# A graph network kernel: early sums cut into even pieces, row search spread out, and unread products on TensorE between the row search and the first transposes

## The reference, cut to what matters

```python
h = relu(layernorm(x))
h = relu(h @ enc_w1.T + enc_b1) @ enc_w2.T + enc_b2
for w in conv_w:                       # 5 layers
    agg = segment_sum((h @ w)[src], dst)
    r, z, n = gates(agg, h)            # a GRU cell, 128 wide
    h = (1 - z) * n + z * h
x = x + sigmoid(relu(relu(h) @ dec_w1.T + dec_b1) @ dec_w2.T + dec_b2)
h = relu(layernorm(x))
x = x + norm_adj @ relu((norm_adj @ h) @ W1.T + b1) @ W2.T + b2
```

## Time and profile before

| | |
|---|---|
| time, median of 3 runs | 748.6 us (747.67 to 749.78) |
| the profiled execution's own time | 747.64 us |
| its span, first to last instruction | 745.6 us |
| PE busy | 722.0 us (97%), 4078 instructions |
| DVE busy | 334.5 us (45%) |
| ACT busy | 314.4 us (42%) |
| POOL busy | 46.3 us (6%) |
| mean granted clock of TensorE | 0.993 of full |

### The profile page before, as it was taken

How to read it: one execution, slowest core, us unless ns; L and a number is a source line. 1 busy time by engine, 2 the same in 40 slices (tenths; PEclk the granted TensorE clock), 3 DMA queues, 4 the chain that set the end, 5 groups by cost and what they waited for, 6 DMA issues and landing times.

```text
span 745.6 us, 9909 instructions
## 1 busy us (share of the span) xinstructions
PE 722.0 (97%) x4078; PEld 393.7 (53%) x4078; DVE 334.5 (45%) x675; ACT 314.4 (42%) x461; POOL 46.3 (6%) x55
## 2 busy tenths in 40 slices
PE   5899999999999999999999999999999999999997
PEld 3566666445444444444444444544445545558886
DVE  7999998434013332122331222656644631122432
ACT  3978777655334444234462333432446411112000
POOL 6320000000000000000000000120002220000000
PEclk7999999999999999999999999999999999999999
DMA  5120000743202232021240212620002000000100
GB/s 165 26 75 2 1 1 2 135 80 62 37 1 47 52 61 53 1 49 37 45 84 0 48 37 38 94 83 2 1 0 85 20 1 1 1 1 2 37 30 26
DMA packets 78795, 28.40 MB, mean 38 GB/s; under 512 B 70340, under 2 KB 77893, under 8 KB 78618
## 3 DMA queue, kind: packets, MB, share of 16 engines
q1 hardware_dynamic: 77786, 26.93, 17.1%
q0 software_dynamic: 240, 0.66, 0.3%
q10 hardware_dynamic: 720, 0.13, 0.1%
HBM read 8.03 MB, written 2.60 MB: 14 GB/s over the span
## 4 chain that ended last, share of the span: by engine, by line
PE 81%; DVE 12%; ACT 2%; DMA 2%; SPq 1%; POOL 1%; issue 1%; ACTq 0%; DVEq 0%
PE PSA L1207 35%; PE PSA L1426 8%; DVE CT L839 6%; PE PSA L1290 5%; PE PSA L1370 5%; PE PSA L1221 3%; PE PSA L1230 3%; PE PSA L1229 3%; PE PSA L1223 3%; PE PSA L1225 3%; PE PSA L1232 3%; PE PSA L1153 2%; PE PSA L1358 2%; PE PSA L1346 1%; DVE stat L804 1%; ACT AT L1533 1%
## 5 line engine op out<-in xcount | busy, mean ns | idle before, releaser
L1207 PE MATMUL PSA<-AT,H 128*128 128x512 fp8e3 (+1 forms) x1472 | 276.0, 347 | 0.8 <-DMA H<-H 0.6
L1207 PEld LDWEIGHTS PSA<-AT,H 128*128 128x128 f16 x1472 | 126.7, 98 | 152.2 <-issue 13.1
L1045 DVE SCALAR_TENSOR_TENSOR rS<-PSA,bias,rS 128x512 f32<-128x512 f32 (+1 forms) x35 | 23.9, 682 | 265.7 <-ACT rS L1600 265.7
L1600 ACT ACTIVATE rS<-PSA,bias 128x512 f32<-128x512 f32 (+1 forms) x35 | 22.1, 632 | 199.6 <-PE PSA L1229 199.6
L839 DVE TENSOR_TENSOR CT<-CT 128x2048 bf16<-128x2048 bf16 x80 | 91.3, 1204 | 0.1
L1533 ACT ACTIVATE AT<-PSA 128x1000 fp8e3<-128x1000 f32 (+1 forms) x79 | 74.4, 1000 | 23.0 <-PE PSA L1153 23.0
L1507 ACT ACTIVATE CTL<-AT 128x3125 fp8e3<-128x3125 fp8e3 (+1 forms) x25 | 69.9, 2796 | 0.0
L1370 PE MATMUL PSA<-CT,H 128*128 128x512 fp8e3 (+1 forms) x336 | 65.5, 352 | 0.3 <-POOL H L747 0.3
L1426 PE MATMUL PSA<-AT,CT 128*128 128x256 f16 x576 | 65.1, 273 | 0.6 <-DVE AT L1007 0.6
L1426 PEld LDWEIGHTS PSA<-AT,CT 128*128 128x128 fp8e3 x576 | 55.4, 98 | 7.3 <-DVE AT L1007 0.8
L1290 PE MATMUL PSA<-AT,H 128*128 128x512 fp8e3 x250 | 59.0, 379 | 0.0
(11 more groups left out here) (173 smaller groups left out, 660.6 us busy)
## 6 DMA issues: line engine op xcount, KB each, us to landing
AT<-scale_scratch SPq DMA_DIRECT2D x1, 1562.5 KB, 6.5
H<-in_x SPq DMA_DIRECT2D x1, 1536.0 KB
out<-AT SPq DMA_DIRECT2D x12, 128.0 KB
comb_scratch<-CT SPq DMA_DIRECT2D x1, 960.0 KB, 5.2
comb<-comb_scratch SPq DMA_DIRECT2D x5, 192.0 KB, 3.0
H<-yS SPq DMA_TRANSPOSE x48, 2.5
H<-in_x SPq DMA_DIRECT2D x1, 512.0 KB, 5.1
CT<-AT SPq DMA_TRANSPOSE x25, 4.0
```

The source lines that it names most:

```text
L1207: last = nc.tensor.matmul(bank[:, 0:w], H16[:, l % 2, t, h, :], AT3[:, t, n0:n0 + w], start=(t == 0 and h == 0), stop=(t == T - 1 and (h = ...
```

## The change

Eight edits are in it:

1. **Unread products.** TensorE makes matmuls of 512 columns on an index row and writes them to a bank that nobody reads: 512 and 384 columns at the start (512 and 512 before), four more between the row search and the first transposes of keys, two more between these and the first transposes of x.
2. **Row search spread out.** Of the 5 groups only k = 0 and 1 are finished at the start. ScalarE copies the products of k = 2 to 4 (`kept`), and VectorE finishes them behind the one-hots of batches 7, 11 and 15 (`ROWS_AT`). The compares are cut in 128, 128 and 384 windows, in place of 128 and 512. The gathers of k = 2 to 4 come later on GpSimd.
3. **Keys later.** `KEYS_AT` is 5, 12, 20, 28 (before 5, 11, 17, 23).
4. **Even pieces.** `PART` cuts the early sums of chunks 2 and 3 in 4, 3, 4, 3, 4, 3, 4 tiles, and of chunk 1 partly in 3.
5. **Tail tile in layer 0.** Its two halves lie in one matmul in layer 0 too: ScalarE writes the encoded last tile twice side by side (`tail_twice`), one transpose brings it to rows 0 to 52 and 64 to 116.
6. **Copies of the tail rows** are made chunk by chunk, 7 times two DMAs, as the chunks fill, ahead of the 5 transposes of `AT` in SyncE's queue, each pair waiting for the pair before it to land.
7. **The copy in layer 0** behind chunk 5 goes away.
8. **The end.** SyncE's wait for the stores comes behind the branch on the flag.

```diff
-        KEYS_AT = {5: 1, 11: 2, 17: 3, 23: 4}
+        KEYS_AT = {5: 1, 12: 2, 20: 3, 28: 4}
+        ROWS_AT = {7: 2, 11: 3, 15: 4}
...
+        EVEN = [0, 4, 7, 11, 14, 18, 21, T]
+        PART.update({23 + 7 * i + g: [(2 + i, EVEN[g], EVEN[g + 1])] for i in range(2) for g in range(7)})
...
-            sp.wait_ge(window_bank_free, NGR)
+            for c in range(NC):
+                n0, w = CH[c][0] * P, width(c)
+                sp.wait_ge(window_bank_free, min(filled(n0 + w), NGR))
+                if c >= 1:
+                    sp.wait_ge(tail_doubled, 32 * c)
+                for p0, p1 in ((0, LR // 16 * 16), (LR // 16 * 16, LR)):
+                    sp.dma_start(AT3[64 + p0:64 + p1, FT, n0:n0 + w], AT3[p0:p1, FT, n0:n0 + w]).then_inc(tail_doubled, 16)
...
-                    if l == 0 and c == 5:
-                        sp.wait_ge(sum_ready, NC)
-                        for p0, p1 in ((0, LR // 16 * 16), (LR // 16 * 16, LR)):
-                            sp.dma_start(AT3[64 + p0:64 + p1, FT, :], AT3[p0:p1, FT, :]).then_inc(tail_doubled, 16)
...
-            sp.wait_ge(output_stored, 16 * (FG + 2))
             sp.wait_ge(flag_ready, 1)
             with sp.If(sp.value_load(flag[0:1, 0:1], min_val=0, max_val=1000) > 0):
+                sp.wait_ge(output_stored, 16 * (FG + 2))
...
+            sp.wait_ge(output_stored, 16 * (FG + 2))
...
+            compared(0, 1)
+            compared(1, SOON)
             dve.wait_ge(window_starts, 4)
             dve.wait_ge(steps_set, 2)
+            first_rows(0)
+            compared(SOON, KW)
+            first_rows(1)
...
-            for _ in range(2):
-                nc.tensor.matmul(PS[EA][:, :], wtop[:, 0:128], wtop[:, 0:512], start=True, stop=True)
+
+            def unread(*widths):
+
+                for n in widths:
+                    nc.tensor.matmul(PS[EA][:, 0:n], wtop[:, 0:128], wtop[:, 0:n], start=True, stop=True)
+
+            unread(512, 384)
...
-                    for h in range(2 if t < FT or l == 0 else 1):
+                    if t == FT and l == 0:
+                        pe.wait_ge(tail_doubled, 32 * (n0 // (TC * P) + 1))
+                    for h in range(2 if t < FT else 1):
...
+            unread(512, 512, 512, 512)
             transposed_keys(0)
+            unread(512, 512)
             encoder(0)
...
+            act.wait_ge(samples_counted, KW)
+            nc.scalar.activation(kept, PSA[0:PW, SOON:KW, 0:NS + 1], ACT.Copy).then_inc(counts_kept, 1)
             copied_keys(0)
```

More of the change, by code:

```diff
@@ L163, in gnn_kernel @@
         inrow = early([PW, KW, NS], F32)
+        kept = early([PW, KW - SOON, NS + 1], F32)
         wstart1 = early([PW, KW], F32)
@@ L733, in _ @@
             pool.memset(AT3[:, :, N:DP], 0.0).then_inc(small_set, 1)
-            pool.memset(H16[:, 0, FT, :, :], 0.0).then_inc(tail_cleared, 1)
+            pool.memset(tail_twice, 0.0).then_inc(small_set, 1)
+            pool.memset(H16[:, 0, FT, :, :], 0.0).then_inc(small_set, 1)
+            for k in range(SOON + 1, KW):
+                gathered(k)
             pool.wait_ge(input_product, (L - 1) * NC)
@@ L786, in _, with compared @@
             dve.wait_ge(window_starts, 1)
[L787 removed]
+            def compared(k0, k1):
+                w0, w1 = k0 * PW, k1 * PW
                 link(nc.vector.tensor_scalar(full[:, w0:w1], wtop[:, w0:w1], ends[0:GP, 1:2], None, ALU.is_lt))
@@ L790, in _, with first_rows @@
                                                ALU.is_lt, ALU.subtract).then_inc(compares_ready, 1)
[L791 to L795, removed]
+            def first_rows(k):
+                if k < SOON:
+                    dve.wait_ge(samples_counted, k + 1)
+                    found = PS[k][0:PW, 0:NS + 1]
+                else:
+                    dve.wait_ge(counts_kept, 1)
+                    found = kept[:, k - SOON, :]
                 link(nc.vector.scalar_tensor_tensor(inrow[:, k, :], found[:, 0:NS], wtop_p[:, k:k + 1], steps, ALU.is_gt, ALU.mult,
@@ L1192, in encoder @@
                         pe.wait_ge(encoded_lo, s - 1)
-                    k = rows(t0)
                     for j in range(nt):
-                        last = nc.tensor.transpose(PS[EB][0:k, j * F:(j + 1) * F],
-                                                   HT[:, (t0 + j) * P:(t0 + j) * P + k], ident[:, :])
+                        cols = HT[:, (t0 + j) * P:(t0 + j + 1) * P] if t0 < FT else tail_twice[:, 0:64 + LR]
+                        last = nc.tensor.transpose(PS[EB][0:cols.shape[1], j * F:(j + 1) * F], cols, ident[:, :])
                     last.then_inc(encoded_transposed, 1)
@@ L1304, in _ @@
                     combine(COMB.index(b))
-                if b in PART:
-                    aggregate_part(*PART[b])
+                for q, t0, t1 in PART.get(b, []):
+                    aggregate_part(q, t0, t1)
             for l in range(L):
@@ L1312, in _ @@
                     if q == AHEAD:
-                        for g in range(BEGUN, NC):
-                            aggregate_part(q, g)
+                        aggregate_part(q, BEGUN, T)
                     if AHEAD < q:
@@ L1578, in encoder @@
                     t0, nt = CH[s - 1]
-                    k = rows(t0)
+                    k = P if s < NC else 64 + LR
                     act.wait_ge(encoded_transposed, s)
-                    if s == NC:
-                        act.wait_ge(tail_cleared, 1)
                     nc.scalar.activation(H16[0:k, 0, t0:t0 + nt, 0, :],
```

82 lines of the change are left out of this document (46 added, 36 removed).

## The result

The changed kernel takes 750.64 us (median of 20 runs, 747.42 to 751.35), the kernel before, on the same chip, 748.45 (20 runs, 747.67 to 749.80). The ratio is 1.002, with a 95% interval from 1.0013 to 1.0027: slower by 0.1 to 0.3%. The prediction was 744.8 with a range up to 747.6.

A forecast was written before the change was run, and what follows sets the result against it. TensorE, busy 722.0 of 745.6 us, was taken as the bound, with its waits. Terms -2.0 (to layer 0's gates), -0.6 (layer change) and -1.2 (end) sum to -3.8: 743.8 profiled, 744.8 as median, range 743.2 to 747.6.

The forecast's parts named there:

- done at 11.2, no delay: At the start: the four unread products run at full clock, 0.86 us each, and do not delay the key transposes.
- The cold rival: At the start: low clock during the four products, one-hots up to 2.9 us later, 746.1 to 747.7 us; chance 0.15.
- The wait at batch 13: TensorE newly waits about 1.7 us for ScalarE's copy of the keys before the encoder's product.
- Ahead of `w13`: Up to the start of `windows(13)`: one-hots begin 0.5 us earlier, `windows(13)` begins 0.4 us later, at 61.9.
- the row search behind one-hots: Groups 2 and 3, at batches 7 and 11, come ahead of batch 13's one-hots: +1.0 us.
- Even pieces: In the early sums: three waits of TensorE for ScalarE to empty a bank go away, 0.8 us each, 2.4 in all.
- `w13` to the gates: From the start of `windows(13)` to the gates of layer 0: new wait, less work and removed waits give -2.4 us.
- Layer 0 to 1: At the change of layers: two DMAs leave SyncE's queue and TensorE's 0.62 us wait for a state transpose goes, -0.6.
- The end: After the last store's issue: flag, branch and what follows run beside the stores, -1.2 us.
- The third rival: At the end: another engine's branch or the stores end the span anyway, no gain there, 746.0 us; chance 0.1.
- The spread: In the batches: a rival had VectorE or ScalarE still hold TensorE, half of 3.0 us lost, 746.3; chance 0.15.
- the rival for slower: In SyncE's queue: late tail copies stop ScalarE and TensorE before the gates, decisive from about 14 us delay; chance 0.06.

The follow-up runs named there:

- e6_before_end: The kernel before with only SyncE's wait for the output stores moved into and behind the branch on the flag: 749.14 us, ratio 1.0003.
- e1_no_unread: The changed kernel without the four unread products and the two behind the key transposes, start products 512 and 512 again: 745.61 us, ratio 0.9973.
- e10_wait_filled: The changed kernel with six more small unread products in TensorE's wait for the keys' copy at batch 13: 748.58 us, ratio 0.9990.
- e7_no_unread_uneven: `e1_no_unread` with the early-sum pieces of chunks 2 to 4 cut as before the change: 747.53 us, ratio 0.9986.
- e5_no_four: The changed kernel without the four unread products ahead of the first key transposes: 745.18 us, ratio 0.9959.
- e8_two: The changed kernel with two in place of four unread products ahead of the first key transposes: 745.74 us, ratio 0.9951.
- e4_before_unread: The kernel before with the unread products alone added, start products 512 and 384: 750.87 us, ratio 1.0029.
- e2_keys11: The changed kernel with the keys of group 2 at batch 11 in place of 12: 746.45 us, ratio 0.9967.
- e9_keys11_filled: `e2_keys11` with four more small unread products ahead of the windows of batch 6: 746.74 us, ratio 0.9977.
- e12_rows_later: `e11_no_four_keys11` with the row search of groups 3 and 4 at batches 14 and 18 in place of 11 and 15: 744.40 us, ratio 0.9938.
- e3_no_unread_keys11: `e1_no_unread` with the keys of group 2 at batch 11 in place of 12: 744.50 us, ratio 0.9947.
- e11_no_four_keys11: `e5_no_four` with the keys of group 2 at batch 11 in place of 12: 744.44 us, ratio 0.9939.

## Why the prediction was wrong, point by point

**The step that failed: "done at 11.2, no delay".** I took the clock in the unread products as full. They ran at half pace, 0.86 a record (the level of 1.2 GHz), until some 13 us and were done at 14.69. The cold rival's 14.7 agrees by two misses that cancel: the products began at 8.77, not 7.8, and took 5.9, not 6.9, since the clock rose within them. One-hots came at 15.60, against 12.83 forecast and 15.7 in the rival: 2.77 of the 7.1 us between the forecast sum, -3.8, and the +3.3 of the spans. I had argued that TensorE was at work ahead of them, as it was ahead of the rise; but the first four records, 3.66 for four, were at half pace themselves. The Trainium skill, "TensorE: Matmul & The Clock Gate", "What's actually happening", has the throttled state as the default and activity as what releases it. The trace agrees: the products began at half pace and ended at 0.43 a record. The 0.15 that I gave the cold rival was too little. The four took 5.9 us, some 2.5 of them while the keys were not ready; the rest put the one-hots off by 2.9 to 3.2 (15.60 for 12.38 to 12.73), and they brought nothing that a run shows.

Why the clock was still low at 8.77 is open, and one rival was not run. In the kernel before it was up at 6 us, as its eight small records in 1.12 show against six in 1.58 here. The change also shortened the products at the start, from 512 and 512 columns to 512 and 384. The small products are slow in 7 of the 9 traces with the shorter start and in 1 of the 5 with the longer one (`e6_before_end`). No kernel has the four behind the longer start; at full pace they would take 3.4 (eight records of 0.43).

**A cost that was not in the sum: the clock behind the new wait.** The wait at batch 13 was forecast as 1.7 and is 1.96. That the clock would fall in it was no term and no rival. Eight matmuls took 3.18 in place of 1.73, and the product ahead of them 0.2 more: 1.65 from 68.36 to 71.97 against `e1_no_unread`'s 64.80 to 66.76 (3.61 and 1.96). The keys' copy itself came 0.6 later after `w13` (3.60 for 3.00). Together these are, to 0.02, the 2.23 by which this stretch exceeds that of `e1_no_unread`. The times of `e10_wait_filled` show the first part to come from the idle stretch. The 0.6 goes with the fall at batch 6: the copy comes 3.53 to 3.60 after `w13` in the three traces with keys at batch 13 and that fall (the changed kernel, `e7_no_unread_uneven`, `e10_wait_filled`), where `windows(13)` takes 1.35 to 1.44, and 3.00 or 3.01 in the three without (`e1_no_unread`, `e5_no_four`, `e8_two`), where it takes 1.12 or 1.13. ScalarE's timeline shows the link. First the copies of batch 12's windows and the copy of the keys in the changed kernel, then in `e1_no_unread`:

```profile
63.57 1.90 ACT L1568 ACTIVATE AT<-PSA 128x1000 fp8e3<-128x1000 f32 x2 [0.78 <-PE PSA L1187]
...
67.79 0.43 ACT L1576 ACTIVATE CT<-PSA 128x256 bf16<-128x256 f32 x1
```

```profile
59.83 1.90 ACT L1566 ACTIVATE AT<-PSA 128x1000 fp8e3<-128x1000 f32 x2 [0.78 <-PE PSA L1187]
...
64.27 0.39 ACT L1574 ACTIVATE CT<-PSA 128x256 bf16<-128x256 f32 x1
```

The fall makes `windows(12)` 0.78 later after the first one-hots (47.30 for 46.52), and `w13` not at all. So ScalarE begins these copies 1.19 ahead of `w13` in place of 1.97, and in the changed kernel it works without a gap from there to the copy of the keys. On the way through ScalarE the fall at batch 6 does cost this 0.6, where the keys are waited for.

**Ahead of `w13`: right.** The start without the four products is 12.38 to 12.73 in six kernels (12.83 forecast), and the row search behind one-hots costs 0.93 up to batch 13 (0.9 forecast). This holds against the profiled run of the kernel before, which has no fall at batch 6. Where the old order has that fall, batch 13 comes 49.03 and 49.30 behind the one-hots (`e4_before_unread`, `e6_before_end`), and the 0.9 is nearly gone.

**Even pieces: right.** Forecast 0.8 for each of three cycles, 2.4; `e7_no_unread_uneven` measures two of them, 1.8 or 0.9 each. The third, chunk 1's, no run takes apart. All of `w13` to the gates was forecast at -2.4 and is -2.43 in `e1_no_unread`: the waits, the new wait and the work as such came out.

**Layer 0 to 1: right, and given back.** TensorE gained 0.78 at this place (it stood 3.05 behind the kernel before ahead of it and 2.27 behind it). At 485.66 it then waits 1.06 for a state transpose, 0.86 more than before, as a transpose of columns kept SyncE's queue for 2.65 us in place of 1.52 ahead of it. Over the kernels with the new order and the even pieces, the stretch from the gates to the last issue is 609.22 without such a wait (`e8_two`), 609.66 to 609.99 with 0.17 to 0.46, and 610.24 to 610.44 with 0.63 to 1.06; `e2_keys11` (0.77 and 609.98) and `e9_keys11_filled` (610.88, with another 0.75 at the first change of layers) lie off this line. So against the 610.18 of the kernel before the term is -0.2 to -1.0 where that wait stays below 0.5, and +0.2 here. Why the issue takes 1.52 in one kernel and 2.65 in another stays open.

**The end: wrong, 0 for -1.2.** I counted SyncE's 1.3 us wait for the stores as part of a chain. `e6_before_end` shows that what follows does not get earlier with the wait elsewhere. The third rival (0.1) had this. What the last 3.5 us consist of, the traces do not show.

**The rivals.** The cold products came true at the full size of their delay. The time that this rival gives, 746.1 to 747.7, was still missed, since the clock fall behind the new wait and the end without gain came on top. I had taken each case alone; more than one held. By the prediction's own measure of 0.3% the result, 0.1 to 0.3% slower, counts as no change, which had 0.19; faster had 0.75. The spread did what its tables say. The tail copies in SyncE's queue, the rival for slower, cost nothing: no wait for `tail_doubled` stands in the trace, and SyncE's next state transpose comes 11.70 us behind the start of the gates in both kernels.

## What to carry to other kernels

Work that only keeps an engine warm must not stand ahead of what the path waits for: price it at the low clock, and look at the record durations for which clock it is. A new wait of two microseconds on TensorE costs more than its length when the clock falls in it (1.65 us more here); look for that after each moved wait, and ask whether independent work can stand in it. Count what a saving at one place is worth only where the next bound lets it through: here VectorE at batch 13 took all that TensorE saved at batch 6, and at batch 21 half of what the earlier keys gave.

## What the hardware showed that was not expected

- **The granted clock's column can say 1.00 while products run at half pace.** From 8 to 15 us it is 1.00 in the changed kernel, where two records in a row take 1.91 at 11.40 and 1.02 at 13.83. At the start of a trace the durations are the safer witness.
- **The same idle stretch lets the clock fall in one run and not in the next.** TensorE waits 2.06 to 2.09 us ahead of batch 6 in twelve of the traces. The clock fell behind it in seven (the changed kernel, `e2_keys11`, `e4_before_unread`, `e6_before_end`, `e7_no_unread_uneven`, `e10_wait_filled`, `e12_rows_later`) and stayed at 1.00 in five (the kernel before, `e1_no_unread`, `e3_no_unread_keys11`, `e5_no_four`, `e11_no_four_keys11`), as it did in `e8_two` with 1.88. The kernel before and `e6_before_end` are the same program up to its end. At batch 13, 1.66 of waiting let it fall in `e8_two` and not in `e1_no_unread` or `e5_no_four`, and 1.96 in the changed kernel and not in `e7_no_unread_uneven`. What decides is not settled.
- **Runs of one kernel probably differ by such falls.** Only one run of each has a trace. Of the 20 runs of the changed kernel the two with a mean granted clock of 1.000 took 747.42 and 747.60; those at 0.991 to 0.995 took 749.03 to 751.35. Even these two are only level with the fastest runs of the kernel before, 747.67.
